# Residual tiles at every step, and the last block of V evicted earlier, in the key stage of a quantised cross-attention layer

## The chip, the cores and the metric

The kernel runs on one core of one Trainium2 chip. The metric is the device time of one execution in microseconds (us). TensorE, VectorE, ScalarE, GpSimd and SyncE are called PE, DVE, ACT, POOL and SP, as in the profile; "the SP queue" is the queue of DMAs that SP issues.

## The reference

One gated layer on x (4 x 512 rows of 512), with a context of 4 x 1024 rows:

```python
q = (layernorm(x) @ Wq + bq) / sqrt(32); kv = ctx @ Wkv + bkv       # 16 heads of 32
q, k = fq_sym(q, row of a head), fq_sym(k, row of a head)           # 127 steps
v = fq_sym(v, over all 4096 keys of a column)
attn = fq_unsigned(softmax(q @ k.T))                                # 2048 rows x 4096 keys a head
x = x + tanh(g_xattn) * (concat_heads(attn @ v) @ Wp + bp)
x = x + tanh(g_ffn) * ffn(layernorm(x))                             # ternary weights w1, w2
```

A column of V is rounded with one step for all 4096 keys, so its largest magnitude must be known before any of it is rounded. `x + tanh(g_xattn) * bp` ("residual with the projection's bias", `xb`) doesn't depend on the attention and is made beforehand.

## The kernel before

There are three stages, each a block of the program that all engines enter and leave together: queries (`project_queries`), keys and values (`project_keys_values`, the key stage), and attention with the rest of the layer (`attend_and_finish`). The change is in the key stage alone.

The key stage goes over 32 tiles of 128 context rows (`KT`). Each engine has a function `step(g)`, and its instructions stand in the order of g; an engine never runs ahead of its own order. In step g

- SP loads context tile g + 2 (`ctx_in`, L501) and a piece of w1 or w2 (`w_in`, L503), stores the rounded piece (`terns`, L508), stores a block of the turned context every fourth step (`ctx_T`, 1 MB, L522), and for key tile g - 4 issues a transpose into the first head's area (L528) and the store of 512 KB (`k_rows`, L530). SP issues these one after another on one queue, and waits before each until its data is ready or its buffer is free;
- PE turns context tile g (four transposes, L558), multiplies tile g - 1 with the key weights (L568), and does one of the four products of a block of 512 values of V (L576, `ps_v`);
- DVE adds the bias to key tile g - 1, finds a head's largest magnitude and scales (L705 to L715), and takes the rounding constant off tile g - 2 (`kq`, L721); after each block of V it takes that block's largest magnitude (`largest_values`, L694);
- ACT evicts the turned context, rounds key tile g - 2 (L624), writes the high and middle bf16 parts of key tile g - 3 (L631, L638), rounds a weight piece, and every fourth step evicts a block of V (`keep_values`, L599);
- POOL subtracts for the rest (`kv_rest`, L676) and writes the low part of key tile g - 3 (L678).

The residual tiles go beside this. x has 16 tiles of 128 rows (`QT`), and `row_tile(g, first)` says which is due in step g. SP loads tile i into `xb[i % 4]` (L513) after the store of tile i - 4 has landed, POOL adds the gated bias (L670), and SP stores it (L517). The stage ends when SP has seen all its stores land (waits that the profile puts at L545).

Of the kernel before, what the change touches and what calls it, by code (L numbers as in the profile page):

```python
# [24 lines left out]
QT = ROWS // P  # L25
KT = KEYS // P
# [20 lines left out]
def after(eng, sem, value):  # L47

    if not isinstance(value, int) or value > 0:
        eng.wait_ge(sem, value)  # L50
# [8 lines left out]
def live(g, total):  # L59

    return not isinstance(g, int) or 0 <= g < total
# [7 lines left out]
def heads(ap):  # L69
    return ap.rearrange("p (h d) -> p h d", d=D)  # L70
# [7 lines left out]
def per_head(ap):  # L78

    return ap.unsqueeze(2).to_broadcast([P, H, D])  # L80
# [307 lines left out]
KEY_BLOCKS = KEYS // BLOCK  # L388
# [27 lines left out]
def key_part(tile, a):  # L416

    return tile[:, :].rearrange("p (h a d) -> p h a d", a=CT, d=D)[:, :, a, :]


def project_keys_values(nc, t, kept, wk, bk, wv, bp, gates, weights_in, gates_in, ctx_in, ctx_loaded, w_in, w_loaded, k_first, q_first):


    with ExitStack() as stack:
# [52 lines left out]
        K_STORES = 2  # L477
        PER_BLOCK = BLOCK // P
        STEPS = KT + 5
        XB_LOAD, XB_ADD, XB_STORE = 2, 4, 6  # L480

        x_tiles = t["x"].rearrange("b (i p) c -> p (b i) c", p=P)
        xb_tiles = t["xb"].rearrange("b (i p) c -> p (b i) c", p=P)

        def row_tile(g, first):

            i = (g - first) // 2
            return i if (g - first) % 2 == 0 and 0 <= i < QT else None

        with nc.Block() as block:  # L490

# [91 lines left out]
            @block.scalar  # L583
            def _(act):
                act.wait_ge(const, 2 + PART_BUFS)
                act.wait_ge(gates_in, 64)

                def round_weights(m):
                    n = m % IN_BUFS
                    act.wait_ge(w_loaded[n], 16 * (m // IN_BUFS + 1))  # L590
                    act.activation(w_in[n][:, :], w_in[n][:, :], ACT.Identity,
                                   bias=up_down[:, 0:1], scale=kept["w_scale"][:, m % 2:m % 2 + 1]).then_inc(w_upped, 1)
                    act.wait_ge(w_upped, m + 1)
                    after(act, tern_stored[m % TERN_BUFS], 16 * (m // TERN_BUFS))
                    act.activation(tern[m % TERN_BUFS][:, :], w_in[n][:, :], ACT.Sign, bias=up_down[:, 1:2]).then_inc(tern_ready, 1)

                def keep_values(j):
                    act.wait_ge(v_ready, j + 1)
                    act.activation(values[:, j * BLOCK:(j + 1) * BLOCK], ps_v[:, :], ACT.Identity,  # L599
                                   bias=kept["bv"][:, 0:1], scale=1.0).then_inc(v_kept, 1)  # L600

                def step(g):

                    if g == 2:
                        act.wait_ge(gates_in, 64)
                        act.activation(kept["gate_tanh"][:, :], gates[:, :], ACT.Tanh).then_inc(gates_ready, 1)

                    j = (g - 8) // PER_BLOCK
                    if g % PER_BLOCK == 0 and live(j, KEY_BLOCKS):
                        keep_values(j)  # L610

                    if live(g, KT):
                        n = g // PER_BLOCK
                        after(act, ctx_turned, g + 1)
                        if g % PER_BLOCK == 0 and n >= 2:
                            act.wait_ge(ctx_stored[n % 2], 16 * (n // 2))
                            act.wait_ge(v_ready, n - 1)
                        at = g % PER_BLOCK * P
                        act.copy(inT[n % 2][:, :, at:at + P], ps_in[g % 2][:, :, :]).then_inc(ctx_kept, 1)  # L619

                    n = g - 2
                    if live(n, KT):
                        act.wait_ge(kv_math, NPER * (n + 1))
                        act.activation(norm[n % 2][:, :], norm[n % 2][:, :], ACT.Identity,  # L624
                                       bias=up_down[:, 0:1]).then_inc(rounded, 1)

                    n = g - 3
                    if live(n, KT):
                        act.wait_ge(kq_ready, n + 1)
                        after(act, k_stored[n % PART_BUFS], 16 * K_STORES * (n // PART_BUFS))  # L630
                        act.copy(key_part(parts[n % PART_BUFS], 0), heads(kq[n % 2][:, :])).then_inc(hi_mid_ready, 1)  # L631

                    if live(g - 1, KT):
                        round_weights(g - 1)

                    if live(n, KT):
                        act.wait_ge(rest_low_ready, 2 * n + 1)
                        act.copy(key_part(parts[n % PART_BUFS], 1), heads(rest[n % 2][:, :])).then_inc(hi_mid_ready, 1)  # L638

                for g in range(STEPS):  # L640
                    step(g)
# [42 lines left out]
            @block.vector  # L684
            def _(dve):
                dve.memset(up_down[:, 0:1], ROUND).then_inc(const, 1)
                dve.memset(up_down[:, 1:2], -ROUND).then_inc(const, 1)
                for i in range(PART_BUFS):
                    dve.memset(parts[i][:, :], 0.0).then_inc(const, 1)
                dve.wait_ge(weights_in, 48)  # L690

                def largest_values(j):
                    dve.wait_ge(v_kept, j + 1)
                    dve.tensor_reduce(v_mag[:, j:j + 1], values[:, j * BLOCK:(j + 1) * BLOCK], AX_X, ALU.max,  # L694
                                      apply_absolute_value=True).then_inc(v_math, 1)

                def step(g):

                    if live(g - 1, KT):
                        r = (g - 1) % 2  # L700
                        done = NPER * (g - 1)
                        dve.wait_ge(k_ready, g)
                        after(dve, kq_ready, g - 2)
                        after(dve, kv_math, done)
                        dve.tensor_tensor(raw[r][:, :], ps_k[r][:, :], bk[:, :], ALU.add).then_inc(kv_math, 1)  # L705
                        dve.wait_ge(kv_math, done + 1)

                        dve.tensor_reduce(small[r][:, 0, :], heads(raw[r][:, :]), AX_X, ALU.max,
                                          apply_absolute_value=True).then_inc(kv_math, 1)
                        dve.wait_ge(kv_math, done + 2)  # L710
                        dve.tensor_scalar(small[r][:, 1, :], small[r][:, 0, :], 1.0 / 127.0, 1e-8, ALU.mult, ALU.max).then_inc(kv_math, 1)
                        dve.wait_ge(kv_math, done + 3)
                        dve.reciprocal(small[r][:, 2, :], small[r][:, 1, :]).then_inc(kv_math, 1)
                        dve.wait_ge(kv_math, done + 4)
                        dve.tensor_tensor(heads(norm[r][:, :]), heads(raw[r][:, :]), per_head(small[r][:, 2, :]), ALU.mult).then_inc(kv_math, 1)  # L715

                    n = g - 2
                    if live(n, KT):
                        dve.wait_ge(rounded, n + 1)
                        after(dve, rest_low_ready, 2 * n - 3)  # L720
                        dve.scalar_tensor_tensor(heads(kq[n % 2][:, :]), heads(norm[n % 2][:, :]), -ROUND, per_head(small[n % 2][:, 1, :]),  # L721
                                                 ALU.add, ALU.mult).then_inc(kq_ready, 1)

                    j = (g - 9) // PER_BLOCK
                    if g % PER_BLOCK == 1 and live(j, KEY_BLOCKS):
                        largest_values(j)

                for g in range(STEPS + 1):
                    step(g)

                dve.wait_ge(gates_ready, 1)
                dve.tensor_scalar(kept["w_part"][:, :], kept["w_step"][:, :], 1.0 / 127.0, None, ALU.mult).then_inc(gates_ready, 1)
                dve.wait_ge(gates_ready, 2)
                dve.tensor_scalar(kept["w2_step"][:, :], kept["w_part"][:, 1:2], kept["gate_tanh"][:, 1:2], None, ALU.mult)
                dve.wait_ge(v_math, KEY_BLOCKS)
                dve.tensor_reduce(v_largest[:, :], v_mag[:, :], AX_X, ALU.max).then_inc(v_math, 1)
                dve.wait_ge(v_math, KEY_BLOCKS + 1)
                dve.tensor_scalar(kept["sv"][:, 0:1], v_largest[:, :], 1.0 / 127.0, 1e-8, ALU.mult, ALU.max).then_inc(v_math, 1)
                dve.wait_ge(v_math, KEY_BLOCKS + 2)
                dve.reciprocal(kept["v_inv"][:, 0:1], kept["sv"][:, 0:1])  # L740
# [1056 lines left out]
```

## Time and profile before

| | |
|---|---|
| median of 3 runs | 1791.2 us (1781.51 to 1794.91) |
| the profiled execution | 1784.63 us, span 1782.8 us |
| key stage in it | 95 to 267.8 us from the span's start |
| busy over the span | PE 86%, DVE 92%, ACT 78%, POOL 74% |

All times inside the profile are counted from the start of its span. A busy share over the span is a mean over three stages of which only the middle one is touched, so the key stage has to be read by itself: which engine has no gaps there, and what it waits for when it has one.

### The profile page before, as it was taken

The page shows a single profiled execution, that of the slowest core. Times are in us where ns is not written, and L with a number is a line of the kernel's source. Part 1 is how long each engine was busy: PE and PEld are TensorE (multiplying, and loading weights), DVE is VectorE, ACT ScalarE, POOL GpSimd, SP SyncE. Part 2 cuts the span into 40 slices and gives each one's busy share as a digit, 9 for nine tenths or more (in the row PEclk, how much of TensorE's full clock was granted, in tenths as well). Part 3 has the DMA queues.
Part 4 walks back from the last instruction along what each step waited for, and adds up shares of the span by engine and source line. Part 5 has one row for each costly group of instructions (what it writes and reads, how often), then busy time and mean ns, then how long its engine had stood idle before and what let it go on. Part 6 is the DMA issues. An engine that isn't in the chain of part 4 may idle for free.

```text
span 1782.8 us, 34656 instructions
## 1 busy us (share of the span) xinstructions
PE 1536.8 (86%) x13190; PEld 753.7 (42%) x13207; DVE 1642.2 (92%) x2214; ACT 1391.6 (78%) x1351; POOL 1319.6 (74%) x1297
## 2 busy tenths in 40 slices
PE   7799968888888888888888987988888887789996
PEld 4344422444444444444444443444444443333332
DVE  7779968999999999999999999999999998388987
ACT  4468857888898878889888888987887886677873
POOL 0156755888989989898988888898998898455342
PEclk9989986999999999999999999999999998899998
DMA  6769986999968999995899989678888876123223
GB/s 208 258 209 365 340 300 127 170 177 170 167 121 142 169 172 181 169 172 106 148 183 166 183 172 155 117 143 160 150 159 135 153 139 145 60 45 86 62 63 83
DMA packets 725640, 286.55 MB, mean 161 GB/s; under 512 B 676121, under 2 KB 680793, under 8 KB 724194
## 3 DMA queue, kind: packets, MB, share of 16 engines
q1 hardware_dynamic: 724098, 281.40, 75.6%
q8 instruction: 105, 1.72, 0.4%
q0 software_dynamic: 704, 1.62, 0.3%
q10 hardware_dynamic: 672, 1.31, 0.2%
q14 instruction: 61, 0.50, 0.1%
HBM read 76.59 MB, written 39.88 MB: 65 GB/s over the span
## 4 chain that ended last, share of the span: by engine, by line
DVE 27%; POOL 27%; issue 13%; PE 13%; ACT 3%; DMA 2%; POOLq 0%; DVEq 0%; ACTq 0%; SPq 0%
DVE att_scaled L1658 25%; POOL att_probsT L1391 22%; PE att_scores L1177 3%; POOL att_low_row L1381 3%; PE att_scores L1117 2%; PE att_ps_o L1197 2%; PE att_scores L1137 2%; POOL att_bias_row L1384 2%; DMA att_pairsT<-att_pairs 1%; ACT att_pairs L1257 1%; PE att_scores L1178 1%; PE att_ps_v L1107 1%; DVE att_v_largest L1627 0%; PE att_scores L1079 0%; ACT att_head_area L1289 0%
## 5 line engine op out<-in xcount | busy, mean ns | idle before, releaser
L1658 DVE TENSOR_SCALAR_CACHE_REDUCE att_scaled<-att_scores,layer_nsq 128x1536 f32<-128x1536 f32 (+1 forms) x768 | 1202.2, 1639 | 18.6 <-PE att_scores L1137 12.7
L1257 ACT ACTIVATE att_pairs<-att_scaled,att_bias_row 128x4096 uint8<-128x4096 f32 x256 | 950.4, 3713 | 144.6 <-DMA att_pairsT<-att_pairs 96.9
L1391 POOL CAST att_probsT<-att_pairsT 128x2048 bf16<-128x2048 uint8 x512 | 953.6, 1891 | 108.4 <-DMA att_pairsT<-att_pairs 98.4
L1137 PE MATMUL att_scores<-first_head_area 96*128 96x512 bf16 x1024 | 297.6, 395 | 96.4 <-DVE att_scaled L1658 79.3
L1137 PE MATMUL att_scores<-att_head_area 96*128 96x512 bf16 x1024 | 289.5, 385 | 66.8 <-DVE att_scaled L1658 63.6
L1098 PEld LDWEIGHTS att_ps_o<-att_v_head,att_probsT 128*128 128x128 bf16 x8192 | 242.7, 96 | 63.3 <-issue 3.7
L1098 PE MATMUL att_ps_o<-att_v_head,att_probsT 128*128 128x32 bf16 x8192 | 245.0, 176 | 0.4 <-ACT layer_o_sum L1248 0.2
L1137 PEld LDWEIGHTS att_scores<-first_head_area 96*128 96x128 bf16 x1024 | 81.5, 99 | 258.4 <-DVE att_scaled L1658 174.6
L1137 PEld LDWEIGHTS att_scores<-att_head_area 96*128 96x128 bf16 x1024 | 80.0, 98 | 215.0 <-DVE att_scaled L1658 152.2
L1079 PE MATMUL att_scores<-att_head_area 96*128 96x512 bf16 x621 | 169.4, 382 | 0.0
L1079 PE MATMUL att_scores<-first_head_area 96*128 96x512 bf16 x570 | 157.7, 386 | 0.0
L568 PE MATMUL kv_ps_k<-kv_weights_wk,kv_inT 128*128 128x512 f32 x256 | 119.3, 610 | 3.0 <-ACT kv_inT L619 3.0
L1381 POOL TENSOR_SCALAR att_low_row<-att_low 128x1 f32<-128x1 f32 x256 | 92.1, 360 | 30.2 <-DVE att_scaled L1658 30.0
L1087 PE MATMUL att_ps_v<-layer_w2T,layer_wp 128*128 128x512 f32 x192 | 100.9, 607 | 5.1 <-ACT layer_w1T L1231 5.0
L1079 PEld LDWEIGHTS att_scores<-att_head_area 96*128 96x128 bf16 x621 | 61.0, 98 | 74.6 <-issue 2.1
L1248 ACT COPY layer_o_sum<-att_ps_o 128x32 f32<-128x32 f32 x256 | 43.8, 171 | 61.0 <-PE att_ps_o L1098 60.9
L1079 PEld LDWEIGHTS att_scores<-first_head_area 96*128 96x128 bf16 x570 | 56.4, 99 | 70.4 <-issue 5.0
L568 PEld LDWEIGHTS kv_ps_k<-kv_weights_wk,kv_inT 128*128 128x128 f32 x256 | 47.7, 196 | 52.3 <-issue 48.9
L1658 DVE DVE_READ_ACCUMULATOR att_scaled<-att_scores,layer_nsq 128x1 f32 x768 | 66.7, 87 | 0.0
L1177 PE MATMUL att_scores<-layer_w1T,att_ints 128*128 128x512 bf16 x246 | 66.0, 390 | 0.8 <-issue 0.6
L1384 POOL TENSOR_SCALAR att_bias_row<-att_low_row 128x1 f32<-128x1 f32 x256 | 48.7, 190 | 22.4
L678 POOL TENSOR_TENSOR kv_parts<-kv_rest,kv_parts 128x512 bf16<-128x512 f32 x32 | 41.8, 1306 | 24.8 <-ACT kv_parts L638 24.8
(181 smaller groups left out, 1634.3 us busy)
## 6 DMA issues: line engine op xcount, KB each, us to landing
layer_w2T<-ctx_T SPq DMA_DIRECT2D x96, 256.0 KB, 3.9
k_rows<-kv_parts SPq DMA_DIRECT2D x32, 512.0 KB, 4.5
q_w_in<-in_L_ffn_w_dram SPq DMA_DIRECT2D x32, 256.0 KB, 2.8
kv_weights_ctx_in<-in_ctx_dram SPq DMA_DIRECT2D x32, 256.0 KB, 4.7
kv_weights_w_in<-in_L_ffn_w_dram SPq DMA_DIRECT2D x32, 256.0 KB, 4.9
ctx_T<-kv_inT SPq DMA_DIRECT2D x8, 1024.0 KB, 6.2
q_x_in<-in_x_dram SPq DMA_DIRECT2D x16, 256.0 KB, 3.7
terns<-kv_tern SPq DMA_DIRECT2D x32, 128.0 KB, 4.3
```

What stands on the lines that cost most here:

```text
L568: last = pe.matmul(ps_k[n % 2][:, :], turned[:, k, at:at + P], wk[:, k, :], start=(k == 0), stop=(k == CT - 1))
L1079: pe.matmul(spare, q_head[slot][:, at:at + P], k_head[slot][:, 0:C], start=True, stop=True)
L1087: pe.matmul(ps_v[:, :], wp[:, k, group * P:(group + 1) * P], ctx_chunk[n % RING], start=(k == 0), stop=(k == CT - 1)).then_inc(chunk_done, 1)
L1098: last = pe.matmul(ps_o[:, 0:D], probsT[r % C_BUFS][:, k, :], v_head[h % 2][:, k * D:(k + 1) * D], start=(k == 0), stop=(k == KT - 1))
L1137: last = pe.matmul(buffer[:, x:x + 512], q_head[slot][:, at:at + P], k_head[slot][:, STARTS[j] + x:STARTS[j] + x + 512], start=True, stop= ...
L1177: pe.matmul(bank, ints_1[i % 2][:, k, :], kept["w1T"][:, k, j:j + C], start=(k == 0), stop=False)
L1248: act.copy(o_sum[:, (r % QT) * C + (r // QT) * D:(r % QT) * C + (r // QT + 1) * D], ps_o[:, 0:D]).then_inc(o_kept, 1)
L1257: act.activation(pairs[g % R_BUFS][:, :].bitcast(U8).rearrange("p (c two) -> p two c", two=2), scaled[u][:, :].rearrange("p (two c) -> p t ...
L1381: pool.tensor_scalar(low_row[:, :], low[u][:, 0:1], low[u][:, 1:2], low[u][:, 2:3], ALU.min, ALU.min).then_inc(low_ready, 1)
L1384: pool.tensor_scalar(bias_row[:, u:u + 1], low_row[:, :], 1.0, LOG255, ALU.mult, ALU.add).then_inc(row_ready, 1)
L1391: pool.tensor_copy(probsT[g % C_BUFS][:, parity * HALF:(parity + 1) * HALF, :].rearrange("p k q -> p (k q)"), bytes_now.rearrange("p (n tw ...
L1658: dve.tensor_scalar(scaled[u][:, STARTS[j]:STARTS[j] + WIDTHS[j]], scores[(g * NCH + j) % 2][:, 0:WIDTHS[j]], kept["nsq"][:, g:g + 1], Non ...
```

## The change

Residual tile i was loaded in step 2 + 2i, added in step 4 + 2i and stored in step 6 + 2i. Now it is loaded in step 2 + i, added in step 4 + i and stored in step 5 + i: loads in steps 2 to 17 instead of 2 to 32, adds in 4 to 19 instead of 4 to 34, stores in 5 to 20 instead of 6 to 36. The eviction of the last block of V moves on ACT from step 36, where it was the last instruction, to step 33, behind the rounding of the last key tile and ahead of the high part of the tile before it. On DVE the search in that block keeps its place in the row, but is written behind the loop. Lines behind the edits have other numbers in the new kernel (L513 is L512 there, L517 is L516).

```diff
@@ -477,15 +477,14 @@
-        XB_LOAD, XB_ADD, XB_STORE = 2, 4, 6
+        XB_LOAD, XB_ADD, XB_STORE = 2, 4, 5
...
         def row_tile(g, first):
 
-            i = (g - first) // 2
-            return i if (g - first) % 2 == 0 and 0 <= i < QT else None
+            return g - first if 0 <= g - first < QT else None
@@ -606,7 +605,7 @@
-                    if g % PER_BLOCK == 0 and live(j, KEY_BLOCKS):
+                    if g % PER_BLOCK == 0 and live(j, KEY_BLOCKS - 1):
                         keep_values(j)
@@ -623,6 +622,9 @@
+                    if g == KT + 1:
+                        keep_values(KEY_BLOCKS - 1)
+
@@ -722,12 +724,13 @@
-                    if g % PER_BLOCK == 1 and live(j, KEY_BLOCKS):
+                    if g % PER_BLOCK == 1 and live(j, KEY_BLOCKS - 1):
                         largest_values(j)
 
-                for g in range(STEPS + 1):
+                for g in range(STEPS - 2):
                     step(g)
 
+                largest_values(KEY_BLOCKS - 1)
```

On the SP queue, steps 6 and 7 of the key stage before; `kv_xb<-in_x_dram` is the load of a residual tile, `xb<-kv_xb` its store:

```order
L501 DMA kv_weights_ctx_in<-in_ctx_dram 128x512
L503 DMA kv_weights_w_in<-in_L_ffn_w_dram 128x512
L508 DMA terns<-kv_tern 128x512
L513 DMA kv_xb<-in_x_dram 128x512
L517 DMA xb<-kv_xb 128x512
L528 DMA_TRANSPOSE first_head_area<-kv_parts 128x1x128
L530 DMA k_rows<-kv_parts 128x2048
L501 DMA kv_weights_ctx_in<-in_ctx_dram 128x512
L503 DMA kv_weights_w_in<-in_L_ffn_w_dram 128x512
L508 DMA terns<-kv_tern 128x512
L528 DMA_TRANSPOSE first_head_area<-kv_parts 128x1x128
L530 DMA k_rows<-kv_parts 128x2048
```

and the same steps of the new kernel, the second of them with the load and the store too:

```order
L500 DMA kv_weights_ctx_in<-in_ctx_dram 128x512
L502 DMA kv_weights_w_in<-in_L_ffn_w_dram 128x512
L507 DMA terns<-kv_tern 128x512
L512 DMA kv_xb<-in_x_dram 128x512
L516 DMA xb<-kv_xb 128x512
L527 DMA_TRANSPOSE first_head_area<-kv_parts 128x1x128
L529 DMA k_rows<-kv_parts 128x2048
L500 DMA kv_weights_ctx_in<-in_ctx_dram 128x512
L502 DMA kv_weights_w_in<-in_L_ffn_w_dram 128x512
L507 DMA terns<-kv_tern 128x512
L512 DMA kv_xb<-in_x_dram 128x512
L516 DMA xb<-kv_xb 128x512
```

Each odd step from 7 to 17 gets both transfers, between the weight pieces and the key tile's DMAs.

At the end of the key stage, ACT before (the last row is the last block of V):

```order
L624 ACTIVATE kv_norm<-kv_norm,kv_up_down 128x512
L631 CAST kv_parts<-kv_kq 128x16x32
L638 CAST kv_parts<-kv_rest 128x16x32
L631 CAST kv_parts<-kv_kq 128x16x32
L638 CAST kv_parts<-kv_rest 128x16x32
L599 ACTIVATE layer_w1T<-kv_ps_v,layer_bv 128x512
```

and in the new kernel, where it stands behind the rounding of key tile 31:

```order
L623 ACTIVATE kv_norm<-kv_norm,kv_up_down 128x512
L598 ACTIVATE layer_w1T<-kv_ps_v,layer_bv 128x512
L633 CAST kv_parts<-kv_kq 128x16x32
L640 CAST kv_parts<-kv_rest 128x16x32
L633 CAST kv_parts<-kv_kq 128x16x32
L640 CAST kv_parts<-kv_rest 128x16x32
```

The eviction is ahead of four casts that it was behind.

On POOL the last rows of the key stage before are

```order
L676 TENSOR_TENSOR kv_rest<-kv_kq,kv_parts 128x512
L678 TENSOR_TENSOR kv_parts<-kv_rest,kv_parts 128x16x32
L670 TENSOR_TENSOR kv_xb<-kv_xb,layer_bp 128x512
L676 TENSOR_TENSOR kv_rest<-kv_kq,kv_parts 128x512
L678 TENSOR_TENSOR kv_parts<-kv_rest,kv_parts 128x16x32
```

and those of the new kernel

```order
L680 TENSOR_TENSOR kv_parts<-kv_rest,kv_parts 128x16x32
L678 TENSOR_TENSOR kv_rest<-kv_kq,kv_parts 128x512
L680 TENSOR_TENSOR kv_parts<-kv_rest,kv_parts 128x16x32
L678 TENSOR_TENSOR kv_rest<-kv_kq,kv_parts 128x512
L680 TENSOR_TENSOR kv_parts<-kv_rest,kv_parts 128x16x32
```

The add between the last two key tiles is gone from here (the last one now stands 16 key tiles before the stage's end).

## Rows read from the trace of the kernel before

**Rows 1.** Stretches of the span, busy time of each engine, clock, DMA share.

```profile
core 0: us, PE busy (x) PEld busy (x) DVE busy (x) ACT busy (x) POOL busy (x), PEclk, DMA share, GB/s
...
95.00:115.00 20.00, 19.61 (x52) 9.44 (x53) 11.11 (x20) 12.87 (x21) 8.86 (x12) 0.87 0.41 115
115.00:217.50 102.50, 102.50 (x303) 49.34 (x301) 95.86 (x136) 84.73 (x137) 71.42 (x55) 1.00 1.00 348
217.50:236.50 19.00, 16.73 (x45) 7.53 (x44) 11.72 (x20) 13.26 (x22) 10.24 (x9) 0.91 1.04 363
...
253.00:267.80 14.80, 0.00 (x0) 0.00 (x0) 4.11 (x9) 3.68 (x6) 6.79 (x7) 0.64 0.64 244
267.80:1782.80 1515.00, 1309.86 (x12486) 642.82 (x12503) 1432.45 (x1806) 1222.10 (x1036) 1202.43 (x1186) 0.97 0.76 140
```

**Rows 2.** Timeline of the SP queue: start, length, what was issued.

```profile
121.03 0.43 SPq L501 DMA_DIRECT2D kv_weights_ctx_in<-in_ctx_dram  x1
...
161.75 0.47 SPq L517 DMA_DIRECT2D xb<-kv_xb  x1
...
198.37 0.43 SPq L501 DMA_DIRECT2D kv_weights_ctx_in<-in_ctx_dram  x1
...
219.78 0.43 SPq L501 DMA_DIRECT2D kv_weights_ctx_in<-in_ctx_dram  x1
```

**Rows 3.** Timeline of PE: start, length, what ran, idle time ahead of it.

```profile
127.92 0.60 PE L558 MATMUL kv_ps_in<-layer_ident,kv_weights_ctx_in 128*128 128x128 f32 x4
...
203.61 0.60 PE L558 MATMUL kv_ps_in<-layer_ident,kv_weights_ctx_in 128*128 128x128 f32 x4
...
225.19 0.66 PE L558 MATMUL kv_ps_in<-layer_ident,kv_weights_ctx_in 128*128 128x128 f32 x4 [2.15 <-DMA kv_weights_ctx_in<-in_ctx_dram]
225.69 5.29 PE L568 MATMUL kv_ps_k<-kv_weights_wk,kv_inT 128*128 128x512 f32 x8
...
232.11 3.60 PE L568 MATMUL kv_ps_k<-kv_weights_wk,kv_inT 128*128 128x512 f32 x8
...
241.14 0.60 PE L558 MATMUL kv_ps_in<-layer_ident,kv_weights_ctx_in 128*128 128x128 f32 x4
```

**Rows 4.** DMA from 120 to 220 us: GB/s in 40 slices, bytes, issue to landing.

```profile
GB/s 344 328 349 309 327 341 352 386 392 356 385 357 323 401 271 424 326 350 352 386 377 388 358 414 300 383 350 334 363 358 362 400 309 360 308 340 236 316 252 439
DMA packets 18351, 35.01 MB, mean 350 GB/s; under 512 B 4880, under 2 KB 7440, under 8 KB 17680
...
kv_weights_ctx_in<-in_ctx_dram SPq DMA_DIRECT2D x21, 256.0 KB, 4.7
...
kv_xb<-in_x_dram SPq DMA_DIRECT2D x10, 256.0 KB, 4.3
xb<-kv_xb SPq DMA_DIRECT2D x10, 256.0 KB, 4.5
```

**Rows 5.** Timeline of POOL, a step with an add.

```profile
205.26 1.35 POOL L678 TENSOR_TENSOR kv_parts<-kv_rest,kv_parts 128x512 bf16<-128x512 f32 x1 [0.82 <-ACT kv_parts L638]
...
206.57 1.72 POOL L670 TENSOR_TENSOR kv_xb<-kv_xb,layer_bp 128x512 f32<-128x512 f32 x1
...
210.13 1.34 POOL L678 TENSOR_TENSOR kv_parts<-kv_rest,kv_parts 128x512 bf16<-128x512 f32 x1 [0.73 <-ACT kv_parts L638]
```

**Rows 6.** Timeline of the stage's end, ACT and POOL.

```profile
254.59 0.62 ACT L631 CAST kv_parts<-kv_kq 128x512 bf16<-128x512 f32 x1 [0.84 <-DVE kv_kq L721]
...
258.27 1.26 POOL L670 TENSOR_TENSOR kv_xb<-kv_xb,layer_bp 128x512 f32<-128x512 f32 x1
259.49 1.15 POOL L676 TENSOR_TENSOR kv_rest<-kv_kq,kv_parts 128x512 f32<-128x512 f32 x1
...
261.20 0.68 ACT L599 ACTIVATE layer_w1T<-kv_ps_v,layer_bv 128x512 f32<-128x512 f32 x1
...
263.21 0.17 DVE L740 RECIPROCAL layer_v_inv<-layer_sv 128x1 f32<-128x1 f32 x1
```

**Rows 7.** Waits of the SP queue, 253 to 268 us: total, times, longest.

```profile
SPq L545 <- DMA k_rows<-kv_parts: 1.5, 1, 1.5
SPq L545 <- DMA xb<-kv_xb: 0.6, 1, 0.6
```

## The prediction, made blind

> **What bounds the kernel now.** I read the busy time by stretches first, because the change touches one stage of three. The attention stage is 1515 us of the 1783 and doesn't change [rows 1]; it begins when the key stage ends, so whatever the key stage gains or loses moves the end by as much. The key stage has four parts. From 95 to 115 us it fills: the DMA engines are only 0.41 busy. From 115 to 217.5 PE has no idle time at all (102.50 of 102.50 us) and the DMA engines' share is 1.00 at 348 GB/s: two resources without a gap. From 217.5 to 236.5 PE is idle for 2.3 us while the DMA share stays at 1.04. The last 14.8 us have no matmul: a chain through DVE, ACT, POOL and SP ends them.
>
> Which of the two full resources is the limit? The reader should put the SP queue's timeline beside PE's. Step 6 of SP (the load of context tile 8) is at 121.03, step 22 (tile 24) at 198.37: 77.34 us for 16 steps, 4.83 a step [rows 2]. PE turns tile 8 at 127.92 and tile 24 at 203.61: 75.69 us, 4.73 a step [rows 3]. PE has its work back to back, and SP, which loads for it, is 0.1 us a step slower. So the load runs ahead by 6.9 us at tile 8 and by 5.2 at tile 24. A context load needs 4.7 us to land [rows 4], so the spare time shrinks from 2.2 to 0.5 us. At tile 28 it is used up: loaded at 219.78, and PE waited 2.15 us for it until 225.19. The eight matmuls behind that wait took 5.29 us where the next eight took 3.60, with the clock down: 1.7 us more. PE bounds the stage up to 222, but with a DMA queue that is already a little too slow.
>
> **Part 1: both residual transfers in steps 6 to 17.** No transfer is added or taken away; 16 loads and 16 stores of 256 KB move to earlier steps. Up to the load of step 22, the old order had issued 10 residual loads and 8 stores, the new one issues 16 and 16: 14 transfers more. Those of step 3 and half of step 5's fall into the part where the DMA engines have idle time [rows 1]; 12 remain. What one costs is not in the trace as such, so I bound it. From above: at the 350 GB/s that the full DMA engines moved [rows 4], 256 KB take 262,144 / 350,000 = 0.75 us. From below: the SP queue's own time for an issue, 0.47 us and a gap of 0.05, 0.52 [rows 2]. I take 0.75, because the DMA engines show no idle time between 115 and 217 [rows 1]; SP, which issues without gaps there, is held back by them.
>
> Then step 22's load is issued 12 x 0.75 = 9.0 us later, at 207.4, and lands 4.7 later, at 212.1, against 203.61 when PE took the tile before. Spare time ahead of PE was only 2.2 us at tile 8, so PE begins to wait at about tile 12 and is then paced at 4.83 + 0.75 = 5.6 us a step. Behind step 20 there are no residual transfers left, the SP queue could go at 4.83 - 0.75 = 4.1 us a step, and PE sets the pace again: tile 31 is turned at 212.1 + 7 x 4.73 = 245.2. Before it was at 241.14 [rows 3], because the old order paid its wait late. So this part costs **+4.1 us**. The bounds: with 0.52 a transfer, 198.37 + 6.2 + 4.7 + 33.1 = 242.4, +1.3; with 14 transfers and the wait for the buffer (rivals) adding 3 us, about +8.
>
> POOL gets an add in each of 16 steps in a row. One step with an add took from 205.26 to 210.13, 4.87 us [rows 5], above PE's 4.73 and below the 5.6 at which the transfers pace the stage. So it is hidden; if that cover is gone, it costs 0.14 x 12 = 1.7 us at most. What lengthens the step is that the add took 1.72 us here against 1.26 for the last one [rows 5, 6], beside work of DVE. The Trainium skill ("SBUF — State Buffer", section "SBUF: two separate sides") says that POOL and DVE lock a shared port pair for a whole instruction. A DVE operation would then stand behind every added add; the row of a step with one add already holds this, so the sum stays.
>
> **Part 2: the stage's end.** The chain there is rest and low part of key tile 31 on POOL, its transpose and store, and the landing. The add at 258.27 stood ahead of `kv_rest` at 259.49 [rows 6]; it is gone: 1.22 us. SP then waited 1.5 us for the key rows' store and 0.6 more for the residual tile's [rows 7]; the second is gone. **-1.8 us**. Bounds: 0, if the cast ahead on ACT comes later by as much, and -2.3, if DVE, which no add crosses any more, is earlier too.
>
> **Part 3: V's last block.** On ACT the eviction takes 0.68 us [rows 6]. It goes in front of the high part of key tile 30, ahead of which ACT sat idle for 0.84 us until DVE's `kq` [rows 6]. So the idle time hides it; without this cover it would push the last two key tiles' casts, +0.7 us. What it frees is the end of DVE's work, 263.21 before [rows 6], perhaps 6 us earlier; but the stage ends at 267.8 with SP's landings, so nothing waits for that: **0**, bounds 0 and +0.7. PE's four products for that block are independent of it.
>
> **Sum.** +4.1 - 1.8 + 0 = +2.3 us. On the profiled execution (1784.63, its span 1782.8) that gives 1786.9. That execution lies 6.6 us below the median of the three runs, 1791.2; my number is made on the median: **1793.5 us**.
>
> **Rivals.**
>
> *The DMA engines have room left.* A share of 1.00 might only mean that packets take longer while PE sets the pace. For it: single slices of 2.5 us reached 424 and 439 GB/s [rows 4]. Against it: the mean of 100 us was 350, and the lead over PE kept shrinking without SP waiting. Then the front-loaded transfers fit, the late wait vanishes, and tile 31 is turned at 203.61 + 7 x 4.73 = 236.7, 4.4 earlier; POOL takes back about 1; with the end, -5.2: 1786.0. The Trainium skill ("HBM Reference", section "Specifications (TRN2)") gives about 425 GB/s for a core that streams alone; by it, an estimate, 1.96 MB of a full step would need 4.6 us, under PE's 4.73. The trace's mean over 100 us is well below that figure. Chance 0.22.
>
> *The SP queue's issue time is the limit.* Then a transfer costs 0.52 and the parts nearly cancel, +1.3 - 1.8: 1790.7, a change that does nothing. For it: SP issues without a gap. Chance 0.20.
>
> *A wait takes the place of the old distance.* A load used to follow its buffer's last store by four steps, now by one: SP issues the store of tile i - 4 and comes to the load of tile i some 5 us later. A store lands after 4.5 us in the median, so some loads would find it still under way, and behind the waiting SP stand the key rows' stores and the next context load. Nine of the twelve reused buffers come in steps without the 1 MB store; at 0.3 us each about +3, less what the engines' backlog covers: 1796.5. Chance 0.13.
>
> *The clock falls, slower than before.* After the wait of 2.15 us PE's next product ran at a lower clock: 1.7 us for one step [rows 3], granted clock 0.91 in that stretch against 1.00 before [rows 1], so part of it at the lower level (1.2 of 2.4 GHz). If the new waits, some 0.9 us in each of about ten steps, did the same to each step, the price would be 10 x 1.7 = 17 us: 1810.5. It decides once single waits come near the 2.15 us seen; they bunch behind the 1 MB stores, where SP's step is longest. Against it: in the filling part PE waited too and the mean was still 0.87. Chance 0.04.
>
> That leaves 0.41 for the forecast.
>
> **How the numbers follow.** The cases lie between 1786 and 1797 except the last. The runs before scatter by 13.4 us, a median of three by perhaps 5 either way; this is wider than the cases. Range 1781 to 1804, which leaves out the clock case and the ends of the scatter. About 1% (18 us) is what a measurement of this kernel can tell from no change. A gain of 18 us would need more than the late wait and the whole end together (4.4 + 2.3), so faster gets 0.02; slower 0.04, the clock; same 0.94.
>
> **What would show it.** Right: PE waits for `ctx_in` between about 145 and 205 us, several times with under 2 us each; context loads at 5.4 to 5.8 us a step there; no wait of 2 us near 222; tile 31 turned at about 245; the last `kv_rest` on POOL right behind the low part of tile 30; from the last product to the next stage 1.8 us less; DVE done with `v_inv` about 8 us before the stage ends; the next stage beginning near 270. Wrong: PE without gaps up to 236 (the engines had room), an SP wait ahead of the residual load (the buffer), or a granted clock under 0.9 between 145 and 205. The number is wrong as a whole if the attention stage, which doesn't change, runs differently by several us.

## The result

Over 20 runs of each, the median went from 1790.11 to 1795.97 us; the ratio is 1.0037, with a 95% interval of 1.0024 to 1.0050. So the change costs 5.9 us by the medians, 0.3%: clear of the scatter, and far under the 1% that the prediction counted as a change. The profiled execution of the new kernel took 1796.00 us, its span 1794.2. That is 11.4 us more than the profiled execution before, about twice the measured loss. Only 3.9 us of it come before the attention stage begins (at 267.83 before, at 271.77 now). The other 7.4 lie in the attention stage, whose code is the same: 1515.0 us before, 1522.4 now. Over the fourteen profiles of this document that stage took 1513.4 to 1522.8 us, short and long in kernels of either kind, so this part is scatter between executions, and the key stage has to be compared by itself.

The stretches of the new kernel's span, in the same cuts as [rows 1]:

```profile
core 0: us, PE busy (x) PEld busy (x) DVE busy (x) ACT busy (x) POOL busy (x), PEclk, DMA share, GB/s
...
115.00:217.50 102.50, 95.38 (x270) 44.50 (x269) 85.49 (x121) 76.36 (x123) 70.77 (x54) 0.97 1.00 347
217.50:236.50 19.00, 19.00 (x58) 9.24 (x57) 16.00 (x25) 15.23 (x25) 9.94 (x8) 1.00 1.02 340
236.50:253.00 16.50, 16.50 (x49) 7.92 (x48) 14.46 (x22) 13.14 (x22) 9.04 (x7) 1.00 0.82 273
```

PE had no idle time from 115 to 217.5 us before. Now 7.1 us of its work are missing there; from 217.5 on it has no idle time, where it had been idle for 2.3. The SP queue, steps 6, 18 and 22 (the loads of context tiles 8, 20 and 24), and what PE did, to be read beside [rows 2] and [rows 3]:

```profile
121.87 0.59 SPq L500 DMA_DIRECT2D kv_weights_ctx_in<-in_ctx_dram  x1
...
189.62 0.46 SPq L500 DMA_DIRECT2D kv_weights_ctx_in<-in_ctx_dram  x1
...
209.11 0.43 SPq L500 DMA_DIRECT2D kv_weights_ctx_in<-in_ctx_dram  x1
```

```profile
148.99 0.66 PE L557 MATMUL kv_ps_in<-layer_ident,kv_weights_ctx_in 128*128 128x128 f32 x4 [2.47 <-DMA kv_weights_ctx_in<-in_ctx_dram]
149.49 5.29 PE L567 MATMUL kv_ps_k<-kv_weights_wk,kv_inT 128*128 128x512 f32 x8
...
172.98 0.66 PE L557 MATMUL kv_ps_in<-layer_ident,kv_weights_ctx_in 128*128 128x128 f32 x4 [3.15 <-DMA kv_weights_ctx_in<-in_ctx_dram]
173.47 5.29 PE L567 MATMUL kv_ps_k<-kv_weights_wk,kv_inT 128*128 128x512 f32 x8
...
194.87 0.66 PE L557 MATMUL kv_ps_in<-layer_ident,kv_weights_ctx_in 128*128 128x128 f32 x4 [1.05 <-DMA kv_weights_ctx_in<-in_ctx_dram]
...
214.42 0.66 PE L557 MATMUL kv_ps_in<-layer_ident,kv_weights_ctx_in 128*128 128x128 f32 x4 [0.41 <-DMA kv_weights_ctx_in<-in_ctx_dram]
...
247.59 0.60 PE L557 MATMUL kv_ps_in<-layer_ident,kv_weights_ctx_in 128*128 128x128 f32 x4
```

SP needs (189.62 - 121.87) / 12 = 5.65 us a step while it carries both residual transfers. PE waits for context tiles four times, for tiles 12, 16, 20 and 24 (at 148.99, 172.98, 194.87 and 214.42). From there it runs at 4.73 us a step to tile 31 at 247.59, 6.4 us later than in the profile before. It is every fourth tile because each of these loads stands behind a 1 MB store, and SP's next two issues are longer there. The transpose and the key rows' store of an ordinary step, and then the same two behind the 1 MB store ahead of tile 12's load:

```profile
135.18 1.14 SPq L527 DMA_TRANSPOSE first_head_area<-kv_parts  x1
136.37 0.59 SPq L529 DMA_DIRECT2D k_rows<-kv_parts  x1
...
139.93 0.46 SPq L521 DMA_DIRECT2D ctx_T<-kv_inT  x1
140.43 2.28 SPq L527 DMA_TRANSPOSE first_head_area<-kv_parts  x1
142.76 1.25 SPq L529 DMA_DIRECT2D k_rows<-kv_parts  x1
```

The waits of the SP queue (total, times, longest), in the stretch from 112 to 290 us, show two things that weren't there or were otherwise:

```profile
SPq L512 <- DMA xb<-kv_xb: 4.1, 7, 1.2
...
SPq L544 <- DMA k_rows<-kv_parts: 2.0, 1, 2.0
```

Seven residual loads had to wait, 4.1 us in all, for the landing of the store issued one step before. And at the stage's end SP waits for the key rows' store alone. The end itself, which answers to [rows 6]:

```profile
259.46 0.67 ACT L598 ACTIVATE layer_w1T<-kv_ps_v,layer_bv 128x512 f32<-128x512 f32 x1
...
260.40 0.62 ACT L633 CAST kv_parts<-kv_kq 128x512 bf16<-128x512 f32 x1 [0.27 <-DVE kv_kq L723]
...
262.81 0.16 DVE L743 RECIPROCAL layer_v_inv<-layer_sv 128x1 f32<-128x1 f32 x1
...
262.97 1.16 POOL L680 TENSOR_TENSOR kv_parts<-kv_rest,kv_parts 128x512 bf16<-128x512 f32 x1 [0.73 <-ACT kv_parts L640]
264.08 1.15 POOL L678 TENSOR_TENSOR kv_rest<-kv_kq,kv_parts 128x512 f32<-128x512 f32 x1
...
268.28 0.58 SPq L529 DMA_DIRECT2D k_rows<-kv_parts  x1
...
271.74 0.33 SPq L997 DMA_DIRECT2D layer_w2T<-ctx_T  x1
```

The eviction of V's last block fits in ACT's idle time, of which 0.27 us are left. `kv_rest` of the last key tile starts as soon as the low part of the one before is written, and the next stage begins at 271.74.

### The profile page after: what moved, and what is told of

It is laid out like the page before. It is cut to its first block, busy times and chain, and to the rows that moved or that the text cites. A ratio compares the mean times of both kernels' runs of the same rounds, so it can differ in the third digit from the quotient of the medians.

```text
span 1794.2 us, 34673 instructions
## 1 busy us (share of the span) xinstructions
PE 1544.9 (86%) x13207; PEld 754.4 (42%) x13207; DVE 1641.8 (92%) x2214; ACT 1391.9 (78%) x1351; POOL 1320.1 (74%) x1297
## 4 chain that ended last, share of the span: by engine, by line
DVE 34%; POOL 22%; PE 13%; issue 11%; ACT 2%; DMA 1%; POOLq 0%; SPq 0%; DVEq 0%; ACTq 0%
DVE att_scaled L1661 32%; POOL att_probsT L1394 18%; PE att_scores L1180 3%; PE att_scores L1120 2%; PE att_ps_o L1200 2%; POOL att_low_row L1384 2%; PE att_scores L1140 2%; POOL att_bias_row L1387 1%; PE att_scores L1181 1%; ACT att_pairs L1260 1%; DVE att_v_largest L1630 1%; PE att_scores L1082 1%; DMA att_pairsT<-att_pairs 1%; PE att_ps_v L1110 1%; ACT att_head_area L1292 0%
## 5 line engine op out<-in xcount | busy, mean ns | idle before, releaser
L1260 ACT ACTIVATE att_pairs<-att_scaled,att_bias_row 128x4096 uint8<-128x4096 f32 x256 | 950.4, 3713 | 149.7 <-DMA att_pairsT<-att_pairs 103.2
L1661 DVE DVE_READ_ACCUMULATOR att_scaled<-att_scores,layer_nsq 128x1 f32 x768 | 62.7, 82 | 0.0
```

The lines of the kernel that those rows point to most:

```text
L1260: act.activation(pairs[g % R_BUFS][:, :].bitcast(U8).rearrange("p (c two) -> p two c", two=2), scaled[u][:, :].rearrange("p (two c) -> p t ...
L1661: dve.tensor_scalar(scaled[u][:, STARTS[j]:STARTS[j] + WIDTHS[j]], scores[(g * NCH + j) % 2][:, 0:WIDTHS[j]], kept["nsq"][:, g:g + 1], Non ...
```

## The experiments

Two lengths are read from every profile: from the first context tile that PE turns (90.4 us in the first profile before) to tile 31, and from there to the first product of the attention stage. They are compared this way because the stage's start moves by up to 2.3 us between executions, and what lies behind it scatters by 9 us. Each kernel but the one before has one profile; the three profiles of that one differ by 3.2 us at tile 31, so a difference of 2 or 3 us between two rows shows little by itself. The ratio is against the kernel before, with its 95% interval.

| kernel | to tile 31 | to the next stage | ratio |
|---|---|---|---|
| before, three profiles | 150.7, 147.5, 149.7 | 177.4, 173.9, 176.5 | 1 |
| the change | 157.5 | 181.7 | 1.0037 (1.0024 to 1.0050) |
| e1 V's block alone | 146.4 | 172.8 | 0.9997 (0.9982 to 1.0012) |
| e2 residual tiles alone | 157.7 | 181.8 | 1.0042 (1.0026 to 1.0059) |
| e3 half the bytes | 151.9 | 176.1 | 1.0012 (0.9993 to 1.0032) |
| e4 two issues for one | 166.3 | 190.4 | 1.0085 (1.0062 to 1.0109) |
| e5 8 residual buffers | 154.0 | 178.1 | 1.0011 (0.9995 to 1.0027) |
| e6 before, deep | 145.7 | 172.6 | 0.9976 (0.9959 to 0.9992) |
| e7 the change, deep | 151.4 | 175.5 | 1.0004 (0.9984 to 1.0023) |
| e8 none beside the 1 MB store | 156.9 | 181.0 | 1.0009 (0.9991 to 1.0027) |
| e9 deep, 8 buffers, later adds | 149.9 | 174.1 | 0.9985 (0.9968 to 1.0002) |
| e10 before, deep, ending earlier | 146.0 | 170.8 | 0.9972 (0.9957 to 0.9987) |

**Which part loses.** e1 leaves the residual tiles as before, e2 leaves V's block as before:

```diff
 # e1, against the changed kernel           # e2 is the reverse of it
-        XB_LOAD, XB_ADD, XB_STORE = 2, 4, 5
+        XB_LOAD, XB_ADD, XB_STORE = 2, 4, 6
-            return g - first if 0 <= g - first < QT else None
+            i = (g - first) // 2
+            return i if (g - first) % 2 == 0 and 0 <= i < QT else None
```

> Only the last block of V is evicted at step 33; the residual tiles stand as before. My theory: the key stage ends with SP's landings, 4 us behind DVE's last reciprocal, and the eviction fits in ACT's idle time, so the time is that of the kernel before within 1 us (ratio 0.9995 to 1.0005), and tile 31 is turned where it was, near 241. Rival: the eviction pushes the casts of the last two key tiles, +0.7 us. Second rival: the shorter end that the changed kernel showed (15.8 us from the last key product to the next stage instead of 18.3) comes from this part; then it is here too, -2 us.

> Only the residual tiles go to every step; V's last block is evicted last, as before. My theory: the whole loss is here, ratio 1.002 to 1.005, tile 31 turned at 246 to 249, and the stage's end is shorter by 2 us or more, since the add and the late store are gone. Rival (the V part gives or costs something): the ratio differs from that of the full change by 0.001 or more.

V's block alone can't be told from no change (the interval runs from 3.2 us less to 2.1 us more); the residual tiles alone lose 1.0042, the whole. From the last key product's start to the next stage e1 needed 21.7 us and e2 19.4, against 22.0 before and 19.5 with both: the shorter end comes from the residual tiles too. What e1 showed besides was unexpected. It issues the same DMAs as the kernel before up to there, and its profile has no late wait: tile 31 comes 4.3 us sooner than in the first profile before.

**Is the late wait always there?** The kernel before was profiled twice more.

> The kernel before once more, for its profile alone. In its first profile PE waited 2.15 us at tile 28, behind a weight piece's issue that took 2.20 us on SP; the run with only V's block moved, which issues the same DMAs, had no such wait. Theory: the spare time there is near nothing, so the wait comes in some executions: tile 31 at 146 to 147 us from the first tile without it, 150 to 151 with it. Rival: it comes in every execution of this kernel.

> The kernel before a third time, as the last one: 146 to 147 us to tile 31 without the late wait, 150 to 151 with it.

The waits of PE for context tiles in the second and in the third profile of the kernel before, and, from the third, the load of tile 24 and a long issue near it:

```profile
222.75 0.66 PE L558 MATMUL kv_ps_in<-layer_ident,kv_weights_ctx_in 128*128 128x128 f32 x4 [0.21 <-DMA kv_weights_ctx_in<-in_ctx_dram]
```

```profile
186.75 0.66 PE L558 MATMUL kv_ps_in<-layer_ident,kv_weights_ctx_in 128*128 128x128 f32 x4 [1.15 <-DMA kv_weights_ctx_in<-in_ctx_dram]
201.44 0.66 PE L558 MATMUL kv_ps_in<-layer_ident,kv_weights_ctx_in 128*128 128x128 f32 x4 [0.28 <-DMA kv_weights_ctx_in<-in_ctx_dram]
207.57 0.66 PE L558 MATMUL kv_ps_in<-layer_ident,kv_weights_ctx_in 128*128 128x128 f32 x4 [1.18 <-DMA kv_weights_ctx_in<-in_ctx_dram]
```

```profile
201.38 0.46 SPq L501 DMA_DIRECT2D kv_weights_ctx_in<-in_ctx_dram  x1
...
202.70 2.39 SPq L508 DMA_DIRECT2D terns<-kv_tern  x1
```

0.2 us in one execution, 2.6 in another, 2.15 and a slow product in the first. The rival, that the same wait comes each time, is refuted; so is my "147 or 150 to 151" in part, since the third lies between. The spare time shrinks to nothing in all three; in e1, with the same DMAs, PE turned tile 24 still 6.0 us behind the issue of its load, where it was 5.2 in the first profile. Then little things decide. In the first profile it was one issue: the weight piece at 207.99 took 2.20 us where others take 0.8, and the load of tile 28 came 21.4 us behind that of tile 24, where e1 needed 19.7. In the third it was not: the long issue at 202.70 stands behind the load of tile 24, which had been issued at 201.38 and for which PE waited until 207.57, 6.2 us later, where a load lands after 4.7 us in the median. The load of tile 8 had also been issued only 6.0 us ahead of PE, instead of 6.9. Why, no run shows. The mean of the three stages before is 175.9 us, so the change makes the stage 5.8 us longer, beside the measured 5.9; with stages that differ by 3.5 us, so close an agreement is partly luck. The first profile alone gave 4.3.

**Bytes, or issues?** e3 moves half the columns with the same instructions (and zeroes the other half of each buffer once, ahead of the first add); e4 the same bytes with twice the instructions.

```diff
 # e3; the store likewise
-  sp.dma_start(xb[i % XB_BUFS][:, :], x_tiles[:, i, :])
+  sp.dma_start(xb[i % XB_BUFS][:, 0:C // 2], x_tiles[:, i, 0:C // 2])
 # e4; the store likewise
+  for q in range(2):
+      sp.dma_start(xb[i % XB_BUFS][:, q * C // 2:(q + 1) * C // 2], x_tiles[:, i, q * C // 2:(q + 1) * C // 2])
```

> The changed kernel with the same DMA instructions in the same order, but each residual load and store moves 256 of the 512 columns, half the bytes; the last stage reads x itself in place of x with the bias, so the projection's bias is left out of the result. POOL's adds are as long as before. Theory (the DMA engines' transfer time is the limit): 32 transfers up to step 22 are 0.37 us shorter each, 12 us in all, so PE waits for no context tile and tile 31 is turned at 236 to 238; the time is 10 us below the changed kernel's and 4 us or more below that of before. Rival (SP's issue time is the limit, 0.52 us each whatever the bytes): as the changed kernel, tile 31 at 246 to 249, ratio near 1.0035.

> The changed kernel with each residual load and each store issued as two DMAs of half the columns: the same bytes, 32 more instructions on the SP queue. Theory (transfer time is the limit): within 2 us of the changed kernel, since SP's issue is hidden behind full engines. Rival (SP's issue time is the limit): 32 x 0.5 = 16 us more work on SP by step 20, so tile 31 is turned some 12 to 16 us later than in the changed kernel, near 260, ratio about 1.011.

**And the buffer?** e5 gives the residual tiles 8 buffers, so that a load waits for a store five steps back.

> The changed kernel with 8 buffers for residual tiles instead of 4, so that a load no longer waits for the store issued one step earlier. In the changed kernel SP waited 4.1 us in 7 pieces for these. If these waits cost what they last, the load of tile 24 is issued 3 to 4 us earlier and the time is 3 to 4 us lower than the changed kernel's (ratio about 1.0015). Theory (the engines have a backlog that covers a wait of SP): 0 to 1 us lower.

The three are read together by the SP queue's pace, from step 6 to step 18, in which each step carries both transfers. First e5, then e3, then e4:

```profile
123.84 0.43 SPq L501 DMA_DIRECT2D kv_weights_ctx_in<-in_ctx_dram  x1
...
187.77 0.73 SPq L501 DMA_DIRECT2D kv_weights_ctx_in<-in_ctx_dram  x1
```

```profile
121.71 0.46 SPq L500 DMA_DIRECT2D kv_weights_ctx_in<-in_ctx_dram  x1
...
185.21 0.43 SPq L500 DMA_DIRECT2D kv_weights_ctx_in<-in_ctx_dram  x1
```

```profile
122.22 0.45 SPq L500 DMA_DIRECT2D kv_weights_ctx_in<-in_ctx_dram  x1
...
197.57 0.43 SPq L500 DMA_DIRECT2D kv_weights_ctx_in<-in_ctx_dram  x1
```

Per step that is 5.33 us (e5), 5.29 (e3) and 6.28 (e4), against 4.81 before, where step 18 was at 178.78, and 5.65 in the changed kernel (5.64 in e2). Before, SP did nothing but issue in these twelve steps: 75 issues took 54.4 of the 57.75 us, with 0.04 us between one and the next, and no wait. So with the buffer wait out of the way, one more transfer a step costs 5.33 - 4.81 = 0.52 us. Half the bytes change that by 0.04. Two more issues a step cost 6.28 - 5.33 = 0.95, or 0.48 each. The price belongs to the issue, not to the bytes: the rival's price, not mine. Tile 31 says the same. Against e5, e4 turned it 12.3 us later, as the rival had it; against the changed kernel only 8.7, since no wait for a residual store is left in e4. e3 turned it 2.1 us sooner than e5, 0.7 of it by shorter waits for residual stores, where my theory had 12 us for the bytes. Two things are not shown. Each plain copy of this stage has 128 rows, and e4 doubles the rows along with the instructions, so the price may be one for the rows. And no run issues the residual transfers from another engine's queue, which would tell SP's own time from a limit behind its queue; that there is one is seen behind the 1 MB stores, where the same issues take twice as long, and e3 leaves those stores as they are.

And the wait for the landing costs 5.65 - 5.33 = 0.32 a step, 3.8 us over twelve steps. In e5 SP's waits for residual stores were 1.1 us instead of 4.1, and tile 31 came 3.6 us sooner (the ratio, 1.0011 against 1.0037, says the same, with intervals that just overlap): my expectation that the engines' backlog covers it was wrong. In e3 these waits were 0.4 us, so part of its gain is the buffer's. The busy share of the DMA engines should be read in this light. The changed kernel, then e3, both from 120 to 185 us:

```profile
120.00:185.00 65.00, 59.34 (x165) 27.50 (x164) 51.89 (x73) 47.81 (x77) 47.85 (x37) 0.95 1.01 353
```

```profile
120.00:185.00 65.00, 61.48 (x181) 28.91 (x180) 58.53 (x82) 51.52 (x83) 53.37 (x39) 1.00 0.99 330
```

e3 moves fewer bytes a second at a share of 0.99. A share of 1.00 was no ceiling: e5 moved 368 GB/s in the same stretch, at 1.03.

**More lead for the context.** e6 and e7 give context tiles and weight pieces 6 buffers, so SP loads them four steps ahead, in the kernel before and in the changed one.

```diff
-IN_BUFS = 4
+IN_BUFS = 6
```

(Four semaphores still serve them in turn; SP waits for a tile's landing four loads later, which is long past.)

> The kernel before with 6 buffers instead of 4 for the context tiles and weight pieces, so that SP loads a tile four steps ahead instead of two. Theory: the wait of 2.15 us at tile 28 and the slow products behind it, 3.9 us together, are gone, tile 31 is turned at 236 to 238, ratio about 0.998. Rival (that wait was an accident of one execution): within 1 us of the kernel before.

> The changed kernel with the same 6 buffers. Theory: the front-loaded transfers are late by 9 to 10 us at tile 24, and four steps of lead hold some 14 us of spare time, so PE doesn't wait; tile 31 at 236 to 238 and the shorter end is kept: 2 us below the deep version of the kernel before, ratio about 0.9965 to 0.997. Rival (what the DMA engines lack shows up anyway, since POOL, ACT and the stores wait in the same queue): tile 31 later than 241, no faster than the kernel before.

e6 did as expected: no wait, 145.7 us. In e7 PE waited for no context tile either, but tile 31 came at 151.4. The waits of e7 from 112 to 250 us name what had been next in line:

```profile
ACT kv_parts L643 <- POOL kv_rest L681: 10.3, 16, 2.5
...
POOL kv_xb L675 <- DMA kv_xb<-in_x_dram: 6.1, 6, 2.3
...
PE kv_ps_v L578 <- ACT layer_w1T L601: 3.0, 3, 1.5
```

The SP queue is as late as before, and now its residual loads come too late for POOL; ACT waits for POOL, and PE for ACT. e9 gives these a lead as well: 8 residual buffers, `XB_LOAD, XB_ADD, XB_STORE = 2, 6, 7` on top of e7. (It also counts the stores of residual tiles and of rounded pieces on two semaphores each, so SP issues such a store only when the one two tiles back has landed; its waits for residual stores were 1.5 us.)

> The deep version of the changed kernel (6 buffers for context tiles and weight pieces), and with it 8 buffers for residual tiles, POOL's add four steps behind the load instead of two (step 6 + i) and the store in step 7 + i. The deep version alone left no wait of PE for a context tile, but POOL waited 6.1 us in six pieces for residual loads, ACT behind POOL and PE behind ACT: tile 31 came 5.7 us later than in the deep kernel before (counted from the first context tile turned). Theory: SP runs late by 8 us or more around step 20 and each thing it loads needs spare steps of its own; with them here, tile 31 comes 146 to 148 us after the first one and the stage is the shortest of those with residual tiles at every step, about 170.5 us to the next stage, ratio about 0.997. Rival (something that can't be given a lead, as the key rows' stores that ACT's casts wait for, is late too): tile 31 at 149 to 152 us.

Tile 31 at 149.9, in the rival's range: POOL's waits for residual loads are gone, and waits for stores take their place. The first line is from the list of waits, the others from the timelines of SP, ACT and PE:

```profile
ACT kv_parts L638 <- DMA k_rows<-kv_parts: 3.4, 5, 1.6
```

```profile
184.03 0.46 SPq L526 DMA_DIRECT2D ctx_T<-kv_inT  x1
...
191.61 0.59 ACT L623 COPY kv_inT<-kv_ps_in 128x512 f32<-128x512 f32 x1 [3.25 <-issue]
...
192.25 3.70 PE L572 MATMUL kv_ps_k<-kv_weights_wk,kv_inT 128*128 128x512 f32 x8 [2.21 <-ACT kv_inT L623]
```

The key rows' stores go through the same late queue, and ACT waits for them before it writes the next key tile's parts. So does the 1 MB store, and it is the one that reached PE. The profile names no releaser for ACT's 3.25 us, but the kernel makes this copy wait for the store issued at 184.03, which reads the same buffer; such stores landed after 4.9 to 7.5 us here, and ACT went on 7.6 us behind the issue. PE waited 2.21 us for the copy, the longest of its waits in this stretch.

**Evened out.** e8 leaves the steps with the 1 MB store free:

```diff
-        XB_LOAD, XB_ADD, XB_STORE = 2, 4, 5
+        XB_LOAD, XB_ADD, XB_STORE = 0, 2, 4
-            return g - first if 0 <= g - first < QT else None
+            free = [n for n in range(2, STEPS) if n % PER_BLOCK != 1]
+            return free.index(g - first) if g - first in free[:QT] else None
```

> The changed kernel, but the steps with the 1 MB store of the turned context carry no residual transfer: a load and a store in three steps of four, in steps 2 to 26 instead of 2 to 20. The changed kernel's waits bunch: 2.47 and 3.15 us behind two of the 1 MB stores, each followed by products of 5.29 us instead of 3.60. Theory: evened out, no single wait of PE comes over 2 us, the products all take 3.60 us, and tile 31 is turned at 242 to 245; the time is 3 to 5 us below the changed kernel's. Rival (only the sum of bytes counts): tile 31 within 1 us of the changed kernel's 247.6.

The waits did even out (nine, the longest 1.89 us, instead of four, the longest 3.15) and the products all took 3.60 us, but tile 31 came at 156.9, 247.5 in this profile, as the rival says. The runs speak for the theory instead: the ratio, 1.0009, is 5 us below the changed kernel's, and below what the profiled stage's 5.1 us would make it (1.0028, just outside the interval). So e8 does not decide. That the slow products add nothing, because while loads set PE's pace they only fill time that PE would have waited, is likely from another pair: e2 had one of them and the changed kernel two, and tile 31 came at 157.7 and 157.5.

**The best version.** e10 is e6 with another list of steps, `loads = [2, 3] + list(range(4, 32, 2))`, adds 2 and stores 4 steps behind; V's block stays last.

> The deep version of the kernel before, with residual loads in steps 2, 3, 4, 6, 8, ... 30, adds two steps and stores four steps behind: every second step again, but ending two steps earlier than before. V's last block stays last. Theory: the last add isn't among the last key tiles' work any more, so the end is 2.5 us shorter, as in all kernels with the full change, and PE waits for nothing: 146 us to tile 31, 170 us from the first context tile to the next stage against 172.6 in the deep kernel before; ratio about 0.996, the fastest of all. Rival: the shorter end needs the residual tiles out of the last ten steps; then 172.5, ratio 0.9975.

The last context tile and the next stage's first product in e10:

```profile
237.94 0.60 PE L561 MATMUL kv_ps_in<-layer_ident,kv_weights_ctx_in 128*128 128x128 f32 x4
...
262.68 2.72 PE L1140 MATMUL att_scores<-first_head_area 96*128 96x512 bf16 x6 [12.99 <-PEq L491]
```

No wait for a context tile, most of the short end (16.4 us from the last key product to the next stage, against 18.6 in e6 and 15.8 in the kernels with the full change), and a ratio of 0.9972: faster than both kernels, 5 us below the one before by the ratio. By its stage it is 1.8 us shorter than e6; by the runs the two can't be told apart.

## Why the prediction was right, and where it wasn't

**The direction and its mechanism held.** The transfers moved forward meet a queue that is already at its limit, PE waits for context tiles between tile 12 and tile 24, and what is late there isn't recovered. Step 22's load was forecast at 207.4 and came at 209.11; tile 24 at 212.1, came at 214.42; the paced steps at 5.6 us, came at 5.65. The wait at 222 vanished. Measured: +5.9 where +2.3 was forecast, so the forecast had less than half of the loss. That the median of 1795.97 us lies in the range says little, since the range was made from the scatter of three runs and is wider than the cases. Of the signs that I had set, one was missed, since two of PE's waits were over 2 us (2.47 and 3.15), and two signs of being wrong came true, SP's wait ahead of the residual load (4.1 us) and an attention stage that ran differently (by 7.4 us, which is scatter).

**The price of a transfer had the wrong reason.** I took 0.75 us from bytes and 350 GB/s, because the DMA engines showed no idle time. e3, e4 and e5 show 0.5 us an issue and next to nothing for the bytes: my lower bound, and the rival "the SP queue's issue time is the limit" as far as its price goes. That the pace came out right was luck: a second thing made up for the price, the wait for the buffer, 0.32 us a step (0.84 in all where I had 0.75). That was the rival "a wait takes the place of the old distance", with chance 0.13 and 3 us; e5 shows 3.6. I had set the two rivals against each other, and both came true together. With the issue's price alone, my own bound had tile 31 at 242.4, or 152.0 from the first tile turned; e5 came at 154.0.

**The term that was mis-sized is part 1, +4.1 us.** It was 6.4 in the same pair of profiles (6.8 from the first tile turned), and 8.2 against the mean of the three profiles before. There are two main reasons. The starting point of the sum, tile 31 at 241.14, came from one execution whose late wait I booked as a saving of 4 us; in the mean of three executions the saving is smaller by 1.4 (149.3 against 150.7), and e1 had no such wait at all. And tile 24 was 2.3 us later than forecast: 1.7 by the issue of its load, in which the buffer's waits are, and 0.6 by its landing (5.3 us instead of 4.7). The last 0.4 is that this profile's first tile was turned 0.4 us sooner.

**Part 2, -1.8, was -2.5.** From the last key product to the next stage: 18.4 before, 15.9 after. The add gives 1.22, the store's landing 0.65 (from the last key rows' issue to the next stage, 4.11 and 3.46); the rest, 0.64, is DVE (it finished scaling the last key tile, `kv_norm`, 3.5 us behind the end of the last key product before, and 2.9 now), named as the lower bound (-2.3, which the measured end is just beyond).

**Part 3, 0, held**, and with it the idle time that covers it: DVE is done 8.8 us before the stage ends, and nothing waits for that.

**The rivals.** "The engines have room left" is right about the engines (up to the 368 GB/s of e5) and wrong in what follows, since SP can't issue fast enough to use it. The clock fell twice, after waits of 2.47 and 3.15 us (granted clock 0.68 over the product from 149.49 on), but e2 has the same length with one fall. Of POOL's adds no wait of PE or ACT in the changed kernel tells that they cost time: ACT waited 1.9 us in all for `kv_rest` from 112 to 250 us. No run takes them out.

## What to carry to other kernels

A queue that issues back to back is a resource like an engine: count its instructions per step, with the time of each, before its bytes, and compare the pace with the engine it feeds. If the feeding queue is slower by even 2%, the lead shrinks in silence, and whatever is moved forward in it delays the loads behind it. Where the queue is late by a whole step, more buffers for one stream only pass the wait to the next (e7, e9); where it is late by little, they are enough (e6). A sum that starts from one execution should not book an accident of that execution (a wait behind one issue of 2 us) as a saving: look for it in a second profile first.

## What the runs showed of the hardware

The DMA engines' busy share is no measure of what is left: 0.99 at 330 GB/s and 1.03 at 368 GB/s, in the same stretch of two kernels (e3 and e5) that differ by half the bytes of some transfers and by four buffers. A DMA instruction of 256 KB (e5) and one of 128 KB (e3) took SP the same, 0.43 to 0.49 us in the median; single ones took 2.2 and 2.4 us without a cause that the trace shows (at 207.99 and at 202.70 us in two profiles of the kernel before). Behind a 1 MB store the next transpose and the next 512 KB store took SP 2.28 and 1.25 us instead of 1.14 and 0.59. A residual store issued one step ahead had often not landed when the next load into its buffer came up, and SP's waits for it added up to 4.1 us. After PE had waited 2.15, 2.47 and 3.15 us, its next eight products took 5.29 us instead of 3.60; after waits of 1.05 and 1.18, and of 2.08 in e5, they didn't.
